# Linear attention by halves of a chunk: scores of each half with itself on eight array tiles, the running state in two steps in SBUF

## What is computed

```python
qkv = xn @ w_attn.T                      # q, k, v: heads of D = 16
q, k = elu(q) + 1, elu(k) + 1
for each chunk of 128 tokens:
    scores = where(tril, q_c @ k_c.T, 0)
    num = scores @ v_c + q_c @ S
    den = scores.sum(-1) + q_c @ z
    S, z = S + k_c.T @ v_c, z + k_c.sum()
y = num / (den + 1e-6)
x + y @ w_proj.T + experts(xn)
```

## Time and profile before

| | us |
|---|---|
| median of 3 runs | 529.89 (527.65 to 530.54) |
| the profiled execution | 526.89 |
| its span, first to last instruction | 525.0 |
| TensorE busy | 481.5 (92%) |
| VectorE busy | 415.3 (79%) |
| ScalarE, GpSimd busy | 279.0, 292.9 |
| steps with attention | 7 to 294 |
| experts | 301 to 525 |

### The profile page before, as it was taken

One profiled execution on the slowest core, in us unless ns is written; L12 is line 12 of the kernel. 1 busy time (PEld: TensorE's weight loads), 2 busy tenths in 40 slices (PEclk: granted clock), 3 DMA queues, 4 the chain that ended last, 5 costly groups with the idle time before them and its releaser, 6 DMA issues.

```text
span 525.0 us, 17478 instructions
## 1 busy us (share of the span) xinstructions
PE 481.5 (92%) x6071; PEld 393.8 (75%) x6071; DVE 415.3 (79%) x901; ACT 279.0 (53%) x535; POOL 292.9 (56%) x482
## 2 busy tenths in 40 slices
PE   4489999998999989999897499999999999999996
PEld 1378888777887778877875378888888888888884
DVE  2678899999999999999969637767767776677775
ACT  0357878877788777887786123333333332333321
POOL 3555877777777777777765433343443434533322
PEclk9789999999999999999999789999999999999999
DMA  8422656746466464664452431222122212220000
GB/s 276 150 82 73 210 151 194 206 150 190 142 203 205 149 197 150 189 204 139 142 180 89 155 97 49 77 66 83 48 73 72 64 57 82 62 68 23 26 16 1
DMA packets 34160, 62.88 MB, mean 120 GB/s; under 512 B 5661, under 2 KB 10014, under 8 KB 33952
## 3 DMA queue, kind: packets, MB, share of 16 engines
q1 hardware_dynamic: 29088, 49.17, 29.7%
q0 software_dynamic: 4992, 12.60, 8.0%
HBM read 51.00 MB, written 13.50 MB: 123 GB/s over the span
## 4 chain that ended last, share of the span: by engine, by line
PE 81%; DVE 9%; issue 4%; ACT 3%; DMA 2%; POOL 1%; DVEq 0%; ACTq 0%; POOLq 0%
PE ps L598 20%; PE ps L611 19%; PE ps L373 7%; PE ps L413 6%; PE ps L442 4%; PE ps L483 4%; PE ps L426 4%; PE ps L456 4%; PE ps L389 3%; PE ps L469 3%; PE ps L567 2%; PE ps L396 2%; PE ps L356 1%; DVE AR L710 1%; PE ps L346 1%
## 5 line engine op out<-in xcount | busy, mean ns | idle before, releaser
L598 PEld LDWEIGHTS ps<-AR,W 128*128 x1872 | 131.5, 99 | 40.1 <-issue 1.3
L598 PE MATMUL ps<-AR,W 128*128 128x128 f16 x1872 | 155.8, 221 | 0.9 <-ACT AR L1146 0.9
L611 PE MATMUL ps<-W,ST 128*128 x624 | 150.4, 326 | 0.3 <-DVE ST L1006 0.3
L1155 ACT ACTIVATE ST<-ST 128x512 f16<-128x512 f32 x78 | 49.2, 630 | 110.5 <-DVE ST L994 110.5
L1262 POOL DMA_INDIRECT out<-AR x39 | 39.7, 1019 | 106.6 <-DVE AR L1026 105.4
L994 DVE SCALAR_TENSOR_TENSOR ST<-ps,TAs,B1S 128x512 f32<-128x512 f32 x78 | 58.3, 748 | 51.5 <-PE ps L598 49.0
L710 DVE TENSOR_TENSOR AR<-ps,CT 128x512 f32<-128x512 f32 x128 | 81.9, 681 | 2.2 <-PE ps L413 2.2
L1213 POOL TENSOR_TENSOR W<-ST,W 128x512 f16<-128x512 f32 x64 | 74.1, 1158 | 15.2 <-ACT W L1105 14.6
L1204 POOL TENSOR_SCALAR AR<-AR,CT 128x256 f32<-128x256 f32 x64 | 58.6, 926 | 20.4 <-DVE AR L704 20.4
L1257 POOL DMA_INDIRECT AR<-scr,AR x39 | 49.9, 1281 | 32.1 <-DVE AR L1026 12.7
L1006 DVE SCALAR_TENSOR_TENSOR ST<-ST 128x512 f16<-128x512 f32 x78 | 53.6, 687 | 15.6 <-ACT ST L1155 15.6
(11 more groups left out here) (144 smaller groups left out, 768.2 us busy)
## 6 DMA issues: line engine op xcount, KB each, us to landing
ST<-in_w SPq DMA_DIRECT2D x128, 256.0 KB, 4.2
scr<-XR SPq DMA_DIRECT2D x32, 256.0 KB, 2.1
XR<-in_x SPq DMA_DIRECT2D x32, 128.0 KB, 4.6
AR<-in_b SPq DMA_DIRECT2D x1, 1024.0 KB, 4.9
AR<-in_wall SPq DMA_DIRECT2D x1, 776.0 KB, 4.4
AR<-scr,AR POOLq DMA_INDIRECT x39, 3.6
out<-AR POOLq DMA_INDIRECT x39
ST<-in_cst SPq DMA_DIRECT2D x1, 576.0 KB, 4.8
```

Source lines behind the costliest of these rows:

```text
L598: a = e.matmul(dst, W[:, off:off + 57472][:, bass.ds(place_of(s), 128)], XT16[s % 2][:, xl * 256 + k * 128:xl * 256 + (k + 1) * 128], star ...
L611: a = e.matmul(PS[4 + s % 2][:, 0:w], src[h % 4][:, fs], W[:, off:off + 57344 + w][:, bass.ds(place_of(s), w)], start=(f == 0 and w == 512 ...
```

## The change

A chunk is treated as two halves of 64 tokens. The scores are made for each half with itself only, 64 x 64 blocks, with 64 weight columns on 32 rows, so that eight array tiles can hold work. What the second half takes from the first comes through the state: `st` makes each half's k times v as separate blocks of 32 rows (only a head pair's own block, no longer all heads against all), in one PSUM bank for each half, and `t32` adds them up in SBUF in two steps, TA after the first half and TB after the second, masking by head parity on the way. `inter` multiplies TB of the chunk before with the first half of q and TA with the second, and it does so for the first chunk of a sequence too (second half only). y is summed in two banks, and `pv` has two parts that swap the banks between the halves. `inter` and `pv` move from p - 3 to p - 4, around `st`. The masks become two operations over two banks each, and `st` waits for the first of them, as it writes beside the scores. q has three buffers, k two. In the queues: `yt1` moves ahead, `vh`, `lg` and `kt` on ScalarE behind `xTc`, `y2` ahead of the later weight quarters, `sums` and `na` of the norm and `t32` before `y` on VectorE, `mxa` behind `yt2`; on GpSimd the root of the norm is split over two steps and `km` is one operation. Small constants and waits that follow from it are left out here.

```diff
@@ -74,7 +64,10 @@
         def sem(name):
             return ctx.enter_context(nc.semaphore(name))
 
-        PS = [ctx.enter_context(nc.psum_tensor(f"ps{i}", [128, 512], F32)) for i in range(8)]
+
+        PSS = [ctx.enter_context(nc.psum_tensor(f"ps{i}", [128, 512], F32)) for i in range(2)]
+        PD = [ctx.enter_context(nc.psum_tensor(f"pd{i}", [128, 1024], F32)) for i in range(3)]
...
-        QK = [ar(512 * i, 512) for i in range(2)]
+        Q = [ar(256 * i, 256) for i in range(3)]
+        K = [ar(o, 256) for o in (768, 1632)]
...
-        S32 = [ar(3072 + 512 * i, 512) for i in range(4)]
+
...
+        S32 = [[ar(3072 + 1024 * i + 512 * j, 512) for j in range(2)] for i in range(2)]
         KT32 = [ar(5120 + 256 * i, 256) for i in range(2)]
         YT1 = ar(5632, 512)
...
+
+        TA, TB = ([ar(7936 + 256 * i + 128 * j, 128).rearrange("p (g o e) -> p g o e", g=2, o=2) for j in range(2)]
+                  for i in range(2))
         WPF = ar(8448, 512).rearrange("p (k n) -> p k n", k=2)
...
 
-        PSC = [PS[i] for i in (2, 3, 4, 7)]
-
-        PMX = PS[1][0:2, 264:392]
-        PMA = PS[1][:, 392:394]
+        PSC = [PS[2 + r][:, 0:256] for r in range(4)]
+
+        PST = [PS[4 + s][:, 256:324].rearrange("p (g o e) -> p g o e", g=2, o=2) for s in range(2)]
...
+        msk = cc(C_MASK, 64).rearrange("p (a b n) -> p a b n", a=1, b=1).broadcast_to((128, 2, 4, 64))
+        par = cc(C_ME, 2).rearrange("p (g o n) -> p g o n", g=1, n=1).broadcast_to((128, 2, 2, 128))
...
+        def qk_of(c):
...
+                    a = e.transpose(PS[0][:, g * 128:(g + 1) * 128], K[c % 2][:, g * 128:(g + 1) * 128], ID32)
                 a.then_inc(S["ktr"], 1)
...
                 if c == 0:
                     e.wait_ge(v_sv, 1)
+                else:
+                    e.wait_ge(s_[0], c)
+                    e.wait_ge(s_[1], c)
+                    e.wait_ge(S["t32"], c)
+                if (c + 2) // 4 >= 1:
+                    e.wait_ge(v_sc, 3 * min((c + 2) // 4, E))
+                n = sum(1 for g in range(NC // 8 - 1) if 8 * g + 13 < c + 3)
+                if n > 0:
+                    e.wait_ge(v_own, n)
+                for g in range(2):
+                    for s in range(2):
+                        t = slice(64 * s, 64 * s + 64)
+                        for r in range(4):
+                            rows = slice(32 * r, 32 * r + 32)
+                            a = e.matmul(PSC[r][t, g * 128:(g + 1) * 128],
+                                         K[c % 2][rows, g * 128 + 64 * s:g * 128 + 64 * s + 64],
+                                         QM[c % 2][rows, g, :, t], start=True, stop=True)
+                a.then_inc(S["sc"], 1)
+
+            def inter(c):
+
+                e.wait_ge(S["t32"], c + 1)
...
-                        e.wait_ge(s_[r], c)
...
+                    e.wait_ge(S["res"], c)
+                first = True
+                for s in range(c % CPB == 0, 2):
+                    state = (TB[(c - 1) % 2], TA[c % 2])[s]
+                    for g in range(2):
+                        o = g * 128 + 64 * s
+                        for r in range(4):
+                            rows = slice(32 * r, 32 * r + 32)
+                            a = e.matmul(PY[r // 2][64 * (r % 2):64 * (r % 2) + 64, o:o + 64], state[rows, g],
+                                         Q[c % 3][rows, o:o + 64], start=first, stop=True, skip_group_check=True)
+                        first = False
+                a.then_inc(S["in"], 1)
+
+            def pv(c, part):
+
+                if part == 0:
+                    e.wait_ge(S["vh"], c + 1)
+                    e.wait_ge(s_[0], c + 1)
+                    e.wait_ge(s_[1], c + 1)
+                else:
+                    e.wait_ge(S["pv0"], c + 1)
                 for g in range(2):
-                    for r in range(4):
-                        rows = slice(32 * r, 32 * r + 32)
-                        a = e.matmul(PSC[r][:, g * 256:(g + 1) * 256], QK[c % 2][rows, 256 + g * 128:384 + g * 128],
-                                     QM[c % 2][rows, g], start=True, stop=True)
-                a.then_inc(S["sc"], 1)
...
-            def inter(c):
-
-                if c % CPB == 0:
-                    return
-                e.wait_ge(S["t32"], n_state(c - 1))
-                e.wait_ge(S["y1"], c)
-                for g in range(2):
-                    for i in range(2):
-                        j = 2 * g + i
-                        a = e.matmul(PS[5][:, j * 128:(j + 1) * 128], T32[:, g, 4 * i:4 * i + 4, :],
-                                     QK[c % 2][:, g * 128:(g + 1) * 128], start=(j == 0), stop=True,
-                                     skip_group_check=True)
-                a.then_inc(S["in"], 1)
...
-            def pv(c):
-                e.wait_ge(S["vh"], c + 1)
-                if c >= 1:
...
-                for i in range(2):
-                    e.wait_ge(s_[2 * i], c + 1)
-                    e.wait_ge(s_[2 * i + 1], c + 1)
-                    for g in range(2):
-                        for t in range(2):
-                            for o in range(2):
-                                j, b = 2 * g + i, 2 * t + o
-                                a = e.matmul(PS[5][32 * b:32 * b + 32, j * 128:(j + 1) * 128],
-                                             V32[c % 2][:, 8 * g + 4 * i + b, :],
-                                             S32[2 * i + t][:, (2 * g + o) * 128:(2 * g + o + 1) * 128],
-                                             start=(c % CPB == 0 and j == 0), stop=True, skip_group_check=True)
-                a.then_inc(S["pv"], 1)
+                    for s in range(2):
+                        t, i = slice(64 * s, 64 * s + 64), (s + part) % 2
+                        o = g * 128 + 64 * s
+                        for b in range(4):
+                            q = (b // 2 * 4 + g * 2 + b % 2) * 64
+                            a = e.matmul(PY[i][32 * b:32 * b + 32, o:o + 64], V32[c % 2][t, 8 * g + 4 * i + b, :],
+                                         S32[c % 2][i][t, q:q + 64], start=False, stop=True, skip_group_check=True)
+                a.then_inc(S["pv" if part else "pv0"], 1)
 
             def st(c):
-                if c % CPB == CPB - 1:
-                    return
+
                 e.wait_ge(S["kt"], c + 1)
                 e.wait_ge(S["vh"], c + 1)
-                if n_state(c) > 1:
-                    e.wait_ge(S["t32"], n_state(c) - 1)
+                e.wait_ge(s_[1], c + 1)
                 for g in range(2):
-                    a = e.matmul(PS[6][:, g * 136:(g + 1) * 136], KT32[c % 2][:, g * 128:(g + 1) * 128],
...
+                    for s in range(2 - (c % CPB == CPB - 1)):
+                        t = slice(64 * s, 64 * s + 64)
+                        for r in range(4):
+                            rows = slice(32 * r, 32 * r + 32)
+                            a = e.matmul(PST[s][rows, g], KT32[c % 2][t, g * 128 + 32 * r:g * 128 + 32 * r + 32],
+                                         V32[c % 2][t, 8 * g + 2 * r:8 * g + 2 * r + 2, 0:17], start=True, stop=True)
                 a.then_inc(S["st"], 1)
...
                 e.wait_ge(S["y1"], c + 1)
-                if c == 0:
-                    e.wait_ge(v_eb1, 1)
-                e.wait_ge(s_[0], min(c + 2, NC))
-                if c >= 1:
-                    e.wait_ge(S["res"], c)
...
-            for p in range(NC + 5):
+            for p in range(NC + 4):
                 if on(p - 3):
                     scores(p - 3)
+                if on(p - 4):
+                    inter(p - 4)
+                    pv(p - 4, 0)
+                if on(p - 3):
                     st(p - 3)
+                if on(p - 4):
+                    pv(p - 4, 1)
                 if on(p - 2):
                     ktr(p - 2)
                 if on(p - 1):
                     xt(p - 1)
+                if on(p - 4):
+                    yt1(p - 4)
                 mx(p)
                 if eights(p, 13) in (0, 1, 2):
...
-                if on(p - 4):
-                    yt1(p - 4)
-                if on(p - 3):
-                    inter(p - 3)
-                mxa(p)
                 if on(p - 1):
                     qk(p - 1)
                 if on(p - 4):
                     yt2(p - 4)
+                mxa(p)
                 if on(p - 1):
                     vg(p - 1)
                 if on(p - 4):
                     pr(p - 4)
-                if on(p - 3):
-                    pv(p - 3)
...
-            def s_mask(c, r):
+                e.scalar_tensor_tensor(qk_of(c), PS[0].rearrange("p (t n) -> p t n", t=2), 1.0, qk_of(c),
+                                       ALU.min, ALU.add).then_inc(S["phi"], 1)
+
+            def s_mask(c, i):
                 e.wait_ge(S["sc"], c + 1)
+                if c >= 2:
+                    e.wait_ge(S["pv"], c - 1)
+                src = PD[i][:, :].rearrange("p (r n) -> p r n", r=2)[:, :, 0:256]
```

(94 more changed lines are left out.)

132 lines of the change are left out of this document (62 added, 70 removed).

## The result

The change makes the kernel slower. The median is 573.9 us (569.1 to 578.8, four runs) against 529.9 us for the kernel before, a ratio of 1.080 (95% interval 1.073 to 1.088). The forecast was 528.7 us with a range up to 545, so the time lies outside it. The ratio leaves out the highest run, 578.8 us, which ran in a slower state of the same kernel. The same kernel measured again beside another set of runs gave 573.2 against 528.6 us, ratio 1.088 (1.081 to 1.094).

The account below looks back on a forecast made before the run. TensorE's own queue was taken to bound plain steps, VectorE a few. Steps with weights -2.8, head +1.0 and tail +0.6 gave -1.2 us: 525.7 profiled, 528.7 us in the median, range 510 to 545.

Parts of the forecast that it names:

- Small matmuls on TensorE: The replaced attention groups take 2.0 us a step against 3.55, so TensorE's work falls from 7.9 to about 6.3.
- rival 4: Tiles of 64 x 32 don't run eight at once on TensorE: groups 3.3 us, loop +0.5, 544 us; chance 0.05.
- rival 1: Small TensorE matmuls in long runs cost 0.032 us each, about 610 us; at half price, 0.016, 545 us; chance 0.10.
- The loop: Path from one step's qk to the next, through the mask, state and ScalarE's copy of k: 7.85 us, before 7.88.
- slack of 0.3: On TensorE, scores, inter and y's first part end 0.3 us before the mask that the state waits for.
- Rivals 2 and 3: Step loop longer, +0.3 a step, 538 us, chance 0.25; or shorter or not closed, 514 us, chance 0.27.
- SyncE: the same transfers ... so nothing.: SyncE makes the same transfers with one loop pass less, weight quarters released a step ahead as before: no cost.
- eight start 0.007 us apart, so 160 do: On TensorE, the 0.007 us between starts of eight weight loads was taken to price the 160 small matmuls.
- The clock: If TensorE's granted clock fell with the new idle time, every TensorE term would double; no chance given.
- The tail: From the last scores to the matmul ending the routing, 11.63 us before: +2.0 and -1.4, net +0.6 us.

Follow-up runs that it names:

- st_late: kt_first with the state moved behind y's transposes, its VectorE additions behind y, and both parts of pv together: 554.1 us, ratio 1.049 to the kernel before.
- kt_first: The changed kernel with the copy of k moved ahead of the copies of v and the logits on ScalarE: 564.7 us, ratio 1.073 to the kernel before.

## Why the prediction failed, point by point

- **Small matmuls on TensorE.** Forecast scores 0.50, inter 0.45, pv 0.25 a part, state 0.28, with 0.3 for changes of shape: 2.0. Measured in st_late, starts to starts: 0.68 + 0.62 + 0.99 + 0.29 = 2.58 (the last in the step from 206.57, with all 32). The tiles do run eight at once (rival 4 is out: the scores took 1.08 in the earlier trace rows). The term that was off most is pv, 0.99 for two parts of 0.25; scores and inter were 0.18 and 0.17 too low, the state was right. Over all it is 2.58 / 160 = 0.016 us for each, rival 1's half price. The Trainium skill's 60 cycles for each (TensorEngine Tiling (Array Packing), section Instruction Overhead), an estimated 4.0 us, was too much: 2.58.
- **The loop.** Forecast 7.85, measured 7.97 to 8.10 where nothing disturbs; idle time in front of qk behind the copy of k, 0.74 us, as written. kt_first shows that this copy is what closes the loop. The other half of the path was wrong: the state was to wait for the mask, and it does so only 4 times, 1.8 us in all. In the step above it starts 179.39 - 177.52 = 1.87 us after the scores with no wait, behind TensorE's own three groups (0.68 + 0.62 + 0.57), which were to take 1.44. So part of the 0.6 us too little for the groups did show here: it used up the slack of 0.3 and is about the 0.1 to 0.2 that is missing. Rivals 2 and 3 are small beside what came.
- **"SyncE: the same transfers ... so nothing."** This is where the reasoning failed. The change adds no transfer to SyncE, but the instructions themselves come in through a queue of their own, and I had no term for it. The change takes the matmuls of a step from 106 to 206 and puts 160 of them in a run. Rival 1 had the right place, long runs of small matmuls, and its half price is what the groups cost, but that put 0.1 to 0.2 us on the loop and not 0.5. What made the loss is another mechanism: a block of 125 that is used up in less than the 2.2 to 2.4 us after which the next one can be used at the earliest. Half of it was to be had before: 2866 matmuls over the 23 packets of the same stretch is 125, and the forecast's own 2.0 us for 160 makes a block 1.6 us long, where blocks had lasted 9.6. That should have been a rival with a price from 0 up. The 2.4 us no row of before shows, as no block was used up early there; the packets took 0.9 to 1.8. My step "eight start 0.007 us apart, so 160 do" used a row of eight weight loads for a run of 160 matmuls.
- **The clock.** The last sentence of the forecast names it and gives it no chance. I counted with 1.5 us of idle time a step, in two parts; the stops were of up to 2.7 at once, and the steps had 40.3 us of low clock.
- **The account of the 38 us in the steps.** The 23 steps with a full clock average 8.68 us, against 8.10 over all steps before: 31 x 0.58 = 18. The eight with low clock sum to 89.8, 89.8 - 8 x 8.68 = 20 more. By cause: about 25 us are stops and, as what is left of the eight steps after their 13.6 us of stops, 89.8 - 8 x 8.1 - 13.6 = some 11 are low clock; 2 or 3 remain. The 11 is a remainder, not a measurement.
- **The tail.** Forecast +0.6, measured +8.8. A stop of 1.7 us before 314.3 is followed by 41.0 us of low clock, through the tail, where work is thin and waits are long; before it was 10.2 us from 296.5. In the view of the tail, the projection takes 2.08 us, where it has 1.09 in the steps above:

```profile
320.66 1.16 PE L424 MATMUL pd<-AR 32*64 32x128 f32 x32
...
339.18 2.08 PE L498 MATMUL pd<-AR 128*128 128x256 f32 x4 [0.47 <-ACT AR L1123]
341.05 1.15 PE L573 MATMUL ps<-ST,XR 128*128 128x39 f16 x13
```

## What to carry to other kernels

Count instructions where a change splits matmuls into many small ones: divide an engine's instructions in a stretch by the packets of its instruction queue, and ask whether any such block is used up faster than the next one comes (here 125 matmuls with their loads, 2.4 us in most stops). What small tiles save in array time they save only up to that rate, and a stop with "issue" in the middle of a group, at constant distances in instructions, is its mark. A stop of TensorE can cost more than its length, since the clock may fall behind it. A shorter loop can give back part of its gain in longer stops, as kt_first did.
